# Tile 1 loaded two places earlier, and the opening of a macaron block in new instruction orders

## The chip, the cores and the metric

One core of one Trainium2 chip. The metric is the device time of one execution in microseconds (us), the median of several runs. The engines are TensorE (PE, with its weight loads as PEld), VectorE (DVE), ScalarE (ACT), GpSimd (POOL) and SyncE (SP), which only issues transfers here.

## The reference

`x` is 16 sequences of 256 tokens of 128 features, 4096 tokens in all. Three residual parts follow each other:

```python
x = x + 0.5 * ffn(layernorm(x))
x = x + attention(layernorm(x))      # layernorm again inside, with gamma and beta
x = x + 0.5 * ffn(layernorm(x))

def ffn(x):        # weights ternary (-1, 0, 1), one scale per output
    h = silu(x @ w1.T * s1) * (x @ w2.T * s2)      # 128 -> 512
    h = gelu(h @ h1.T * sh1)                       # 512 -> 512
    h = gelu(h @ h2.T * sh2)                       # 512 -> 512
    return h @ w3.T * s3                           # 512 -> 128

def attention(h):  # running sums along the sequence
    keys, values = h @ Wk.T + bk, h @ Wv.T + bv
    w = exp((keys @ Wka.T + bka) / sqrt(128)); w = w / cumsum(w)
    return cumsum(w * keys) * values
```

## The kernel before

The tokens are worked in 8 tiles of 512 (`TOK`). Each tile goes through the first ffn (steps T = 0 to 7), the attention, and the second ffn (T = 8 to 15), so there are 16 ffn tiles, worked by a software pipeline of 16 steps. All is held in SBUF. In step i TensorE works the second and third layers of tile i (`p2`, `p3`, 32 products of 128x128 by 512 columns each), the first layer of tile i+1 (`p1`, 16 products) and the last layer of tile i-1 (`p4`, 8 products). A hidden size of 512 is four chunks m = 0 to 3 of 128 rows; `p2.0` is output chunk 0.

Every activation is split into a high part, rounded to the matmul's format (`high`, ScalarE, `act_hi`), and the rest (`low`, VectorE, `act_lo`), and every product is made twice, once for each. Weights are used in a copy cast to that format (`hi`). As this is exact only for weights without low bits, the kernel *looks* at all weights (`bits:h1.0` is the look at quarter 0 of `h1`: a maximum on VectorE, L801, or a sum on ScalarE, L713, over the low 16-bit halves), collects the looks in a flag in three steps (`raise` on VectorE L811, `sum` on TensorE L556 and L564, `copy` to an integer on VectorE L816), and TensorE loads the flag (L655) and branches (L656) ahead of each of its parts "first", "second" and "rest".

The first layer of one chunk runs: `p1.m` on TensorE writes a gate and an up bank; `tanh.m` on ScalarE (L684) reads the gate; `gate.m` (L855) and `up.m` (L867) on VectorE make the product in `full1`; `high1.m` (ScalarE L689) and `low1.m` (VectorE L877; in the opening chunks 1 and 2 on GpSimd, L375) make its two parts. The layer norm of a tile is `stats` (L825), `aggr` (L832) and `veps` (L839, L840) on VectorE, a power on GpSimd (L362, L364), `z` on ScalarE (L726), four transposes `t` on TensorE (L462) and `t` on ScalarE and VectorE, which make `xn_hi` and `xn_lo`. Of gelu, `gelu2.m` (L701) reads the bank of `p2.m`. `dt` adds the result of `p4` to the residual in `xt_sb`. The fold (L625, L626) multiplies two attention weights together once.

Each engine executes its queue in order. The orders are written out by hand as strings: `START` (tile 0's norm, then its first layer), `SECOND_LAYER` (TensorE's products of `p2` of tile 0 one by one: `p2ahi.0` is input chunk a, high part, output chunk 0), `FIRST_STEP` (the rest of step 0), `ORDER` (three kinds of steps with attention and, as its fourth entry, one without, used in steps 1 and 14) and `LAST_STEP`. A tile is counted `AHEAD`: `stats`, `aggr`, `veps`, `zwait` and `z` belong to tile i+2, `t`, `p1`, `tanh`, `gate`, `up`, `high1` and `low1` to tile i+1. An order decides only when an instruction is issued; its semaphore waits stay as they are. So what stands behind a waiting instruction waits too.

In tile 0's second layer the banks are `gate_ps` and `up_ps`, so `p2ahi.0` waits for `gate.0`, `p2ahi.1` for `up.0`, `p2ahi.2` for `gate.1` and `p2ahi.3` for `up.1`; in tile 1's first layer `p1.2` waits for `gelu2.0` and `gelu2.1`, and `p1.3` for `gelu2.2` and `gelu2.3`, which read its banks.

Transfers of the opening are issued from SP and from ACT: on SP the first half of tile 0, `w1`, `h1.0`, `h1.2`, half of `h1.3`, tile 1 (`xload(1, 2, s_x1t)`), `h2`, `w3`; on ACT the other half of tile 0, `w2`, the vectors, `h1.1` and the other half of `h1.3`.

Of the kernel before, what the change touches and what calls it, by code (L numbers as in the profile page):

```python
# [10 lines left out]
ACT = mybir.ActivationFunctionType  # L11
# [22 lines left out]
        "t vec:s1 bits:h1.1 bits:h1.3 tanh.0 tanh.1 tanh.2 high1.0 tanh.3 high1.1 zwait z.0 z.1 high1.2 bits:h2.0 "  # L34
        "high1.3 1:t",
# [3 lines left out]
        "flag:copy1 bits:h1.0 t vec:scales bits:h1.2 stats flag:raise2 aggr gate.0 veps flag:copy2 up.0 gate.1 "  # L39
        "up.1 low1.0 gate.2 up.2 gate.3 up.3 bits:h2.1 low1.3 1:t",  # L40
# [8 lines left out]
)  # L49
FIRST_STEP = {  # L50
# [52 lines left out]
def macaron_block(nc, x, xt, w1t, w2t, h1t, h2t, w3t, wkt, wkat, wvt, wkn, vecs, out, seq):  # L103
# [895 lines left out]
```

## Time and profile before

| | us |
|---|---|
| time before, median of 3 runs (376.67 to 377.38) | 376.67 |
| the profiled execution | 376.7 |
| its span, first to last instruction | 374.9 |
| busy: TensorE, weight loads | 368.0, 291.9 |
| busy: VectorE, ScalarE, GpSimd | 321.9, 314.1, 52.6 |

The page gives the busy share of each engine and its slices. TensorE is busy in all but the first and the last slices; its granted clock is 0.998 of full speed as a mean. Matmuls are pipelined, so one lasts longer (0.39 us) than the step from one to the next. In a row of the timeline, the bracket behind an instruction tells how long its engine was idle before it and what ended that.

### The profile page before, as it was taken

What the parts mean: (1) busy time and instruction counts of PE and PEld (TensorE: products, weight loads), DVE (VectorE), ACT (ScalarE), POOL (GpSimd) and SP (SyncE); (2) the same over time, 40 slices, a digit from 0 to 9 for tenths busy, and PEclk for the clock granted to TensorE, in tenths of its full rate; (3) what the DMA queues carried; (4) which work ended last, traced back from release to release, by engine and by line L of the source; (5) the groups of instructions that cost most, each with busy time, mean ns of one, the idle gap of its engine ahead of it and who ended that gap; (6) DMA issues with size and microseconds to landing.
All of it is one profiled execution on the core that took longest, in us unless ns stands there. A gap on an engine that the chain in (4) does not pass through costs nothing.

```text
span 374.9 us, 5278 instructions
## 1 busy us (share of the span) xinstructions
PE 368.0 (98%) x1662; PEld 291.9 (78%) x1662; DVE 321.9 (86%) x713; ACT 314.1 (84%) x549; POOL 52.6 (14%) x67
## 2 busy tenths in 40 slices
PE   7999999999999999999999999999999999999996
PEld 2678888787787877778788787778877778788885
DVE  5898787999999799999988999989799999976733
ACT  4999699989977999798699979967998998686763
POOL 3531101202101202201021120102101210020000
PEclk9999999999999999999999999999999999999999
DMA  7760000000000000000000000000000000000001
GB/s 246 277 265 1 2 0 0 1 2 1 0 2 0 1 2 2 2 0 1 2 0 1 2 1 28 2 28 1 2 29 0 0 30 1 30 1 28 2 0 58
DMA packets 4494, 9.81 MB, mean 26 GB/s; under 512 B 625, under 2 KB 1905, under 8 KB 4209
## 3 DMA queue, kind: packets, MB, share of 16 engines
q1 hardware_dynamic: 3744, 8.65, 6.3%
q10 hardware_dynamic: 720, 0.80, 0.6%
q8 instruction: 15, 0.25, 0.2%
q14 instruction: 15, 0.11, 0.1%
HBM read 7.35 MB, written 2.10 MB: 25 GB/s over the span
## 4 chain that ended last, share of the span: by engine, by line
PE 95%; DMA 2%; DVE 1%; SPq 1%; issue 0%; ACT 0%; ACTq 0%
PE hid_ps L449 60%; PE gate_ps L449 8%; PE y_ps L449 7%; PE up_ps L449 7%; PE xt_ps L462 3%; DMA x_sb<-x 2%; PE y_ps L462 2%; PE xt_ps L632 2%; PE xt_ps L629 2%; PE xt_ps L635 2%; PE up_ps L507 1%; PE gate_ps L507 1%; DVE gate L855 0%; PE xt_ps L449 0%; DVE xt_sb L924 0%
## 5 line engine op out<-in xcount | busy, mean ns | idle before, releaser
L449 PE MATMUL hid_ps<-act_hi,hi_h 128*128 128x512 f32 x480 | 195.6, 408 | 0.0
L449 PE MATMUL hid_ps<-act_lo,hi_h 128*128 128x512 f32 x480 | 186.8, 389 | 0.0
L877 DVE TENSOR_TENSOR act_lo<-full,act_hi 128x512 fp32r<-128x512 f32 x185 | 122.2, 683 | 26.8 <-ACT act_hi L708 24.3
L701 ACT ACTIVATE full<-hid_ps,vec 128x512 f32<-128x512 f32 x123 | 84.4, 686 | 34.9 <-PE hid_ps L449 31.2
L449 PEld LDWEIGHTS hid_ps<-act_hi,hi_h 128*128 128x128 f32 x480 | 90.1, 188 | 22.4 <-issue 4.1
L449 PEld LDWEIGHTS hid_ps<-act_lo,hi_h 128*128 128x128 f32 x480 | 90.2, 188 | 22.1 <-issue 4.3
L708 ACT ACTIVATE act_hi<-full 128x512 fp32r<-128x512 f32 x127 | 78.5, 630 | 2.3
L362 POOL TENSOR_TENSOR rstd<-veps,half 128x4 f32<-128x4 f32 x24 | 35.2, 1467 | 272.5 <-DVE veps L840 272.5
L855 DVE SCALAR_TENSOR_TENSOR gate<-tanh,gate_ps 128x512 f32<-128x512 f32 x60 | 40.6, 679 | 9.2 <-ACT tanh L684 8.6
L684 ACT ACTIVATE tanh<-gate_ps,s_half 128x512 f32<-128x512 f32 x60 | 40.8, 686 | 8.2 <-PE gate_ps L449 8.2
L867 DVE SCALAR_TENSOR_TENSOR full<-up_ps,s_half,gate 128x512 f32<-128x512 f32 x60 | 44.2, 742 | 0.9
L689 ACT ACTIVATE act_hi<-full 128x512 fp32r<-128x512 f32 x60 | 37.3, 621 | 0.2
L940 DVE RECIPROCAL rcsum<-csum 128x256 f32<-128x256 f32 x16 | 27.9, 1743 | 0.0
L449 PE MATMUL gate_ps<-xn_hi,hi_w 128*128 128x512 f32 x59 | 24.7, 419 | 0.0
L726 ACT ACTIVATE z<-y_ps,nmr,rstd 128x128 f32<-128x128 f32 x64 | 24.0, 460 | 0.8 <-POOL nmr L364 0.8
L449 PE MATMUL y_ps<-act_hi,hi_w 128*128 128x512 f32 x60 | 24.2, 403 | 0.0
L449 PE MATMUL y_ps<-act_lo,hi_w 128*128 128x512 f32 x60 | 23.5, 392 | 0.0
L449 PE MATMUL gate_ps<-xn_lo,hi_w 128*128 128x512 f32 x59 | 23.0, 390 | 0.0
L449 PE MATMUL up_ps<-xn_lo,hi_w 128*128 128x512 f32 x59 | 23.0, 390 | 0.0
L449 PE MATMUL up_ps<-xn_hi,hi_w 128*128 128x512 f32 x59 | 23.0, 390 | 0.0
L825 DVE BATCH_NORM_STATS2 stats<-y_ps 128x6 f32<-128x128 f32 x64 | 14.2, 285 | 0.0
L462 PE MATMUL xt_ps<-ident,z 128*128 128x128 f32 x90 | 13.6, 273 | 0.0
(159 smaller groups left out, 397.8 us busy)
## 6 DMA issues: line engine op xcount, KB each, us to landing
xt_sb<-xt SPq DMA_DIRECT2D x1, 2048.0 KB, 10.9
out<-xt_sb SPq DMA_DIRECT2D x7, 256.0 KB, 2.0
x_sb<-x SPq DMA_DIRECT2D x1, 1536.0 KB, 6.6
raw_h<-h2t SPq DMA_DIRECT2D x4, 256.0 KB, 7.3
raw_h<-h1t SPq DMA_DIRECT2D x2, 256.0 KB, 5.9
raw_w<-w2t ACTq DMA_DIRECT2D x1, 256.0 KB, 4.0
raw_w<-w1t SPq DMA_DIRECT2D x1, 256.0 KB, 3.8
raw_h<-h1t ACTq DMA_DIRECT2D x1, 256.0 KB, 6.7
```

Source lines behind the costliest of these rows:

```text
L362: eng.tensor_tensor(rstd[:, :], veps[:, :], half[:, :], ALU.pow).then_inc(s_pow, 1)
L449: mm = eng.matmul(ps, w, a, start=(first and n == 0), stop=(last and n == len(seq_) - 1))
L462: mm = eng.transpose(dst[:, j * P:(j + 1) * P], src[:, j * P:(j + 1) * P], ident[:, :])
L684: eng.activation(tanh_b[m % 2][:, :], gate_home(T, m)[:, :], ACT.Tanh, scale=s1_half[:, m:m + 1]).then_inc(s_tanh, 1)
L689: eng.activation(act_hi[first_act(T)][:, m, :], full1[m % 2][:, :], ACT.Copy).then_inc(s_hi[1], 1)
L701: eng.activation(full23[m % 2][:, :], home23(n, T, m)[:, :], ACT.Gelu, scale=col("sh1" if n == 2 else "sh2", m)).then_inc(s_gelu[n], 1)
L708: eng.activation(act_hi[n][:, m, :], full23[m % 2][:, :], ACT.Copy).then_inc(s_hi[n], 1)
L726: zz = eng.activation(z[:, j * P:(j + 1) * P], norm_blk(kind, t, j), ACT.Identity, bias=nmr[:, j:j + 1], scale=rstd[:, j:j + 1])
L855: eng.scalar_tensor_tensor(gate_b[m % 2][:, :], tanh_b[m % 2][:, :], 1.0, gate_home(T, m)[:, :], ALU.add, ALU.mult).then_inc(s_gate, 1)
L867: eng.scalar_tensor_tensor(full1[m % 2][:, :], up_home(T, m)[:, :], s12_half[:, m:m + 1], gate_b[m % 2][:, :], ALU.mult, ALU.mult).then_in ...
L877: eng.tensor_tensor(act_lo[a][:, m, :], full[m % 2][:, :], act_hi[a][:, m, :].bitcast(F32), ALU.subtract).then_inc(s_lo[n], 1)
L940: eng.reciprocal(rcsum[:, b], csum[:, b]).then_inc(s_rc, 1)
```

## The change

Five things, all of them in the order of instructions; no operation is added or taken away.

1. SP issues the load of tile 1 behind `h1.0`, ahead of `h1.2` and half of `h1.3`.
2. `START`: VectorE looks at `h1.0` and makes the scales ahead of copy 1 and `t`; the statistics of tile 1 come ahead of the look at `h1.2`; `raise2` comes behind `gate.0`. ScalarE makes its scale ahead of `t` and looks at `h1.3` behind `tanh.0`, at `h2.0` behind `tanh.1` and at `h2.1` (which was VectorE's) ahead of `high1.3`; `z` is cut in two halves around `high1.1` and `tanh.3`.
3. `SECOND_LAYER`: the products of tile 0's second layer in another order; one of them (`p2clo.3`) moves behind the sum of flag 3.
4. `FIRST_STEP`: TensorE makes the fold behind `p1.3`; ScalarE's `tanh.2` and `tanh.3` come earlier; VectorE's `veps` comes ahead of `low2.0`.
5. `ORDER`, fourth entry (steps 1 and 14): `p4` behind `p2.3`; on ScalarE `t` ahead of `gelu2.0`; on VectorE `stats` first and `dt` late.

```diff
@@ -31,36 +31,36 @@
     ),
     "ACT": (
         "hi:w1 hi:w2 zwait z",
-        "t vec:s1 bits:h1.1 bits:h1.3 tanh.0 tanh.1 tanh.2 high1.0 tanh.3 high1.1 zwait z.0 z.1 high1.2 bits:h2.0 "
-        "high1.3 1:t",
+        "vec:s1 t bits:h1.1 tanh.0 bits:h1.3 tanh.1 bits:h2.0 tanh.2 high1.0 zwait z.0 high1.1 tanh.3 z.1 high1.2 "
+        "bits:h2.1 high1.3 1:t",
     ),
     "DVE": (
         "stats aggr veps bits:w1 bits:w2 norm",
-        "flag:copy1 bits:h1.0 t vec:scales bits:h1.2 stats flag:raise2 aggr gate.0 veps flag:copy2 up.0 gate.1 "
-        "up.1 low1.0 gate.2 up.2 gate.3 up.3 bits:h2.1 low1.3 1:t",
+        "bits:h1.0 vec:scales flag:copy1 t stats bits:h1.2 aggr gate.0 flag:raise2 veps up.0 flag:copy2 gate.1 "
+        "up.1 low1.0 gate.2 up.2 gate.3 up.3 low1.3 1:t",
     ),
 }
 
 
 SECOND_LAYER = (
-    "p2ahi.0 p2ahi.1 p2ahi.2 p2ahi.3 p2alo.1 p2alo.3 p2bhi.3 p2alo.0 p2alo.2 p2bhi.0 p2bhi.2 t p2blo.0 p2bhi.1 "
-    "p2blo.1 p2blo.3 p2chi.0 p2blo.2 p2clo.0 p2dhi.0 p2chi.1 p2chi.2 p2clo.1 p2dlo.0 p2chi.3 p2dhi.1 p2clo.3 "
-    "p2clo.2 p2dlo.1 flag:sum3 p1.0 p2dhi.2 p2dhi.3 p1.1 p2dlo.2 p2dlo.3"
+    "p2ahi.0 p2ahi.2 p2ahi.3 p2ahi.1 p2alo.2 p2alo.1 p2alo.0 p2alo.3 p2bhi.1 p2bhi.2 p2bhi.0 p2bhi.3 t p2blo.0 "
+    "p2blo.2 p2chi.0 p2chi.2 p2blo.1 p2chi.1 p2clo.0 p2clo.2 p2dhi.0 p2clo.1 p2dlo.0 p2blo.3 p2chi.3 p2dhi.1 "
+    "p2dlo.1 flag:sum3 p1.0 p2dhi.2 p1.1 p2clo.3 p2dlo.2 p2dhi.3 p2dlo.3"
 )
 FIRST_STEP = {
-    "PE": "p1.2 0:fold p1.3 p3.0 p3.1 p3.2 p3.3",
-    "ACT": "bits:w3 bits:h2.3 gelu2.0 high2.0 gelu2.1 tanh.0 high2.1 tanh.1 gelu2.2 gelu2.3 high2.2 high1.0 high2.3 tanh.2 "
-           "high1.1 gelu3.0 tanh.3 high3.0 high1.2 gelu3.1 high3.1 high1.3 gelu3.2 zwait z gelu3.3 high3.2 high3.3",
-    "DVE": "bits:h2.2 flag:raise3 stats aggr flag:copy3 low2.0 gate.0 low2.1 gate.1 up.0 up.1 "
-           "low2.2 low2.3 low1.0 gate.2 low1.1 up.2 gate.3 veps up.3 low3.0 low3.1 low1.2 low1.3 0:fold low3.2 "
-           "low3.3",
+    "PE": "p1.2 p1.3 0:fold p3.0 p3.1 p3.2 p3.3",
+    "ACT": "bits:w3 bits:h2.3 gelu2.0 high2.0 gelu2.1 tanh.0 high2.1 tanh.1 gelu2.2 gelu2.3 high2.2 tanh.2 high2.3 "
+           "tanh.3 high1.0 zwait high1.1 gelu3.0 high3.0 high1.2 gelu3.1 high3.1 high1.3 gelu3.2 z gelu3.3 high3.2 "
+           "high3.3",
+    "DVE": "bits:h2.2 flag:raise3 stats aggr flag:copy3 veps low2.0 gate.0 low2.1 gate.1 up.0 up.1 low2.2 low2.3 "
+           "gate.2 low1.0 low1.1 up.2 gate.3 up.3 low3.0 low1.2 low3.1 low1.3 0:fold low3.2 low3.3",
 }
 ORDER = {
     "PE": (
         "p2.0 a:u t p2.1 p2.2 p1.0 p1.1 p2.3 p1.2 a:t p4 p1.3 a:logits u p3.0 p3.1 a:keys p3.2 p3.3",
         "p2.0 t b:u p2.1 p2.2 p1.0 p1.1 a:values p2.3 b:t p4 p1.2 p1.3 u b:logits p3.0 p3.1 b:keys p3.2 p3.3",
         "p2.0 p2.1 t p2.2 p4 p1.0 p1.1 p2.3 b:values p1.2 p3.0 u p3.1 p1.3 p3.2 p3.3",
-        "p2.0 t p2.1 p2.2 p1.0 p1.1 p4 p2.3 p1.2 p1.3 p3.0 p3.1 p3.2 p3.3",
+        "p2.0 t p2.1 p2.2 p1.0 p1.1 p2.3 p4 p1.2 p1.3 p3.0 p3.1 p3.2 p3.3",
     ),
     "ACT": (
         "gelu2.0 high2.0 t gelu2.1 high2.1 gelu2.2 tanh.0 high2.2 tanh.1 a:zwait a:z tanh.2 gelu2.3 high1.0 "
@@ -71,8 +71,8 @@
         "gelu3.3 high3.3 zwait z",
         "gelu2.0 t gelu2.1 high2.0 high2.1 gelu2.2 high2.2 tanh.0 tanh.1 gelu2.3 high2.3 high1.0 tanh.2 gelu3.0 "
         "high3.0 high1.1 gelu3.1 tanh.3 high3.1 high1.2 gelu3.2 high3.2 high1.3 zwait z gelu3.3 high3.3",
-        "gelu2.0 t gelu2.1 high2.0 tanh.0 high2.1 tanh.1 gelu2.2 high2.2 gelu2.3 high1.0 high2.3 high1.1 tanh.2 "
-        "zwait tanh.3 gelu3.0 high3.0 gelu3.1 high1.2 high3.1 gelu3.2 high3.2 high1.3 z gelu3.3 high3.3",
+        "t gelu2.0 gelu2.1 high2.0 high2.1 gelu2.2 tanh.0 tanh.1 high2.2 gelu2.3 high1.0 high1.1 tanh.2 high2.3 "
+        "gelu3.0 tanh.3 high3.0 gelu3.1 zwait high3.1 high1.2 gelu3.2 high3.2 high1.3 z gelu3.3 high3.3",
     ),
     "DVE": (
         "a:stats low2.0 a:aggr t a:veps low2.1 gate.0 up.0 gate.1 up.1 low2.2 gate.2 low1.0 low2.3 dt up.2 low1.1 "
@@ -82,8 +82,8 @@
         "low1.3 b:recip.0 low3.2 b:recip.1 low3.3 b:weight",
         "t b:weight_keys low2.0 b:pool low2.1 dt gate.0 low2.2 up.0 gate.1 b:values low2.3 b:dt gate.2 up.1 stats "
         "low1.0 low3.0 aggr up.2 gate.3 veps low1.1 up.3 low1.2 low3.1 low1.3 low3.2 low3.3",
-        "t stats gate.0 low2.0 up.0 gate.1 up.1 aggr low2.1 veps dt low2.2 low2.3 low1.0 gate.2 gate.3 up.2 low1.1 "
-        "low3.0 up.3 low1.2 low3.1 low3.2 low1.3 low3.3",
+        "stats t aggr low2.0 low2.1 gate.0 up.0 gate.1 up.1 veps low1.0 low2.2 low1.1 low2.3 gate.2 up.2 gate.3 "
+        "low3.0 up.3 low1.2 low3.1 low1.3 dt low3.2 low3.3",
     ),
 }
 
@@ -322,9 +322,9 @@
             eng.dma_start(x_sb[:, 0:TOK // 2], x[:, 0:TOK // 2]).then_inc(s_x0, 16)
             eng.dma_start(raw["w1"][:, :], w1t).then_inc(s_w1, 16)
             eng.dma_start(part(raw, "h1", 0), h1t[:, 0:HID]).then_inc(s_h1[0], 16)
+            xload(1, 2, s_x1t)
             eng.dma_start(part(raw, "h1", 2), h1t[:, 2 * HID:3 * HID]).then_inc(s_h1[2], 16)
             eng.dma_start(h1_end(raw["h1"], 0), h1_end(h1t, 0)).then_inc(s_h1[3], 16)
-            xload(1, 2, s_x1t)
             for k in range(MC):
                 eng.dma_start(part(raw, "h2", k), h2t[:, k * HID:(k + 1) * HID]).then_inc(s_h2[k], 16)
             eng.dma_start(raw["w3"][:, :], w3t).then_inc(s_w3, 16)
```

## Rows read from the trace of the kernel before

**Rows 1.** Busy time by stretch: bounds, length, engines (instructions), clock, DMA share, GB/s.

```profile
13.66:26.52 12.86, 12.80 (x58) 9.80 (x59) 12.27 (x28) 12.43 (x26) 5.84 (x7) 1.00 0.83 309
26.52:360.00 333.48, 333.48 (x1499) 267.44 (x1498) 295.70 (x640) 287.55 (x499) 41.04 (x44) 1.00 0.02 6
```

**Rows 2.** Chain that ended last: start us, length us, what.

```profile
3.06 7.05 DMA x_sb<-x
...
26.68 9.08 PE hid_ps L449 x40
35.77 0.44 PE xt_ps L462 x4
```

**Rows 3.** Timeline of TensorE: start us, us, what [idle before <-releaser].

```profile
8.41 0.36 PE L478 MATMUL gate_ps<-xn_hi,hi_w 128*128 128x256 f32 x1 [0.56 <-ACT xn_hi L762]
...
9.20 0.28 PE L478 MATMUL gate_ps<-xn_lo,hi_w 128*128 128x256 f32 x1
...
11.13 0.19 PE L564 MATMUL y_ps<-ones,inexact 128*1 128x1 f32 x2 [0.59 <-DVE inexact L811]
11.25 0.50 PE L449 MATMUL hid_ps<-xn_hi,hi_w 128*128 128x512 f32 x1
...
13.66 0.47 PE L507 MATMUL gate_ps<-act_hi,hi_h 128*128 128x512 f32 x1 [0.22 <-ACT act_hi L689]
...
25.05 0.38 PE L625 MATMUL xt_ps<-wka,wk_rows 128*128 128x128 f32 x2
...
25.52 0.47 PE L449 MATMUL gate_ps<-xn_hi,hi_w 128*128 128x512 f32 x1
```

**Rows 4.** Timeline of VectorE, 7 to 12 us, same columns.

```profile
7.27 0.14 DVE L816 CAST flag_i<-hid_ps 1x1 int32<-1x1 f32 x1
7.34 0.66 DVE L801 TENSOR_REDUCE bits<-raw_h 128x1 f32<-128x512 uint16 x1
...
10.14 0.87 DVE L825 BATCH_NORM_STATS2 stats<-x_sb 128x6 f32<-128x128 f32 x4 [0.65 <-DMA x_sb<-x]
10.93 0.14 DVE L811 TENSOR_REDUCE inexact<-bits 128x1 f32<-128x6 f32 x1
...
11.35 0.65 DVE L855 SCALAR_TENSOR_TENSOR gate<-tanh,gate_ps 128x512 f32<-128x512 f32 x1
```

**Rows 5.** Timeline of SyncE, issue of the quarter h1.2.

```profile
2.12 0.43 SPq L325 DMA_DIRECT2D raw_h<-h1t  x1
```

**Rows 6.** DMA issues between 2.5 and 2.7 us: KB each, us to landing.

```profile
raw_h<-h1t SPq DMA_DIRECT2D x1, 256.0 KB, 6.6
...
raw_h<-h1t SPq DMA_DIRECT2D x1, 128.0 KB, 6.0
```

**Rows 7.** TensorE's load of flag 1, L655, 7 to 8 us.

```profile
L655 PEldq TENSOR_LOAD <-flag_i x1: 495/495/495, 7.4 to 7.4; - x1
```

**Rows 8.** Timeline of ScalarE, same columns as rows 3.

```profile
7.88 0.38 ACT L762 ACTIVATE xn_hi<-y_ps 128x256 fp32r<-128x256 f32 x1
...
9.67 0.64 ACT L713 ACTIVATE csum<-raw_h 128x512 f32<-128x512 uint16 x1
...
10.30 1.25 ACT L684 ACTIVATE tanh<-gate_ps,s_half 128x512 f32<-128x512 f32 x2
...
14.81 1.64 ACT L726 ACTIVATE z<-x_sb,nmr,rstd 128x128 f32<-128x128 f32 x4
...
24.70 0.68 ACT L701 ACTIVATE full<-up_ps,vec 128x512 f32<-128x512 f32 x1
```

**Rows 9.** Timeline of GpSimd, low1.2 of tile 0.

```profile
17.05 1.30 POOL L375 TENSOR_TENSOR act_lo<-full,act_hi 128x512 fp32r<-128x512 f32 x1 [0.78 <-ACT act_hi L689]
```

**Rows 10.** Warm-up: weight loads at first, then the last matmuls.

```profile
2.94 0.13 PEld L642 LDWEIGHTS y_ps<-ones 128*1 128x1 f32 x1 [0.30 <-issue]
3.36 0.13 PEld L642 LDWEIGHTS y_ps<-ones 128*1 128x1 f32 x1 [0.30 <-issue]
...
6.51 0.59 PE L642 MATMUL y_ps<-ones 128*1 128x256 f32 x2
```

## The prediction

> **What bounds the kernel now.** I read the stages first, then TensorE's own rows, then the engines that feed it. From 26.5 us to the last tile TensorE is never idle: 333.48 us busy out of 333.48, at a granted clock of 1.00 [rows 1]. A moved step there can gain only if it ends a wait that no row shows. The chain of waits says the same and gives the pace: 40 products of 512 columns in 9.08 us, 0.227 each [rows 2]. Time can come or go only in the opening. Between 13.66 us (first product of the second layer, `p2ahi.0`) and 26.52 (first of `p3.0`) stand 32 products of the second layer and 16 of tile 1's first layer, 48 x 0.227 = 10.90, with four transposes (0.44 [rows 2]), the flag sum (11.13 to 11.25, 0.12) and the fold (25.05, about 0.4 [rows 3]): 11.86. The stage takes 12.86 [rows 1], so about 1.0 us of it is waiting, in pieces of 0.1 to 0.2. Before it TensorE waits twice in the open: 0.56 us for `xn_hi` at 8.41, and 0.59 at 11.13 for `inexact`, which VectorE makes only after the statistics of tile 1 [rows 3]. Those waited for their data: 0.65 us idle until 10.14, when the transfer of 7.05 us from 3.06 landed [rows 2, 4]. That is the wait the change aims at.
>
> I follow the change until `p3.0` starts and add the difference to the median, 376.67 (the profiled execution took 376.7, with a span of 374.9, so the two are one).
>
> **The load.** Tile 1 is issued two places earlier, in the slot of 2.12 us, whose transfer landed after 6.6 us, at 8.7; the half quarter issued right behind it took 6.0, and landed at 8.6 [rows 5, 6]. I take 8.7 for tile 1. The three transfers together are the same bytes, so the last of them lands at 10.1 as the last does now. Bounds for tile 1: 8.6 to 10.1. The Trainium skill ("DMA: Bandwidth & Descriptors", "Queues, rings and completion order") says that completion is not FIFO per issuing engine; here the half quarter issued second did land first by 0.1, so the page and these rows agree, and by that rule alone the place in the queue would promise nothing (the second rival has its price).
>
> **Flag 1 comes later.** Copy 1 runs on VectorE at 7.27 and the look at h1.0 behind it (0.66) [rows 4]. Now the look and the two small scales come first. An instruction here starts 0.07 before the one in front of it ends (7.27+0.14 against 7.34). So: look 7.27, scales 7.86 and 7.93, copy 8.00 to 8.14 instead of 7.41. TensorE reads the flag with a load of 0.495 us that begins as the copy ends [rows 7], and then branches; today `p1.0` starts 8.41-7.41 = 1.00 after the copy's end. New: 9.14, that is +0.73. The profile names `xn_hi` as the releaser; its first half is read from 7.85 on and the second ends at 7.88+0.38 = 8.26 [rows 8]. If that end was the limit, `p1.0` needs of the flag no more than what remains when 8.26-7.41 is taken off, and could start as early as 8.14+0.44 = 8.6, +0.17. Bounds +0.17 to +0.73. I take +0.73, as the load fills the gap.
>
> **Looks and tanh.** ScalarE reaches `tanh.0` at 10.30 today because it first looks at h1.3 (9.67 to 10.30, 0.63) [rows 8]. The new order puts that look behind. The first gate tile is ready 9.20+0.28-8.41 = 1.07 after `p1.0` starts [rows 3], so `tanh.0` starts (0.04 behind TensorE's end) at 9.14+1.07+0.04 = 10.25: no change, since what the order gives the late flag takes. VectorE: `t` to 8.8, statistics 8.75 to 9.6, look at h1.2 (landed between 8.7 and 10.1) ends by 10.2 to 10.8, aggregates 0.33, done by 11.0 at the latest; `gate.0` needs `tanh.0` (10.25+0.67) and starts at 10.95, 0.4 earlier than 11.35. But `raise2` now stands behind `gate.0` and needs the look at h1.3, which ScalarE makes after `tanh.0`: 10.25+0.57+0.63+0.09 = 11.55 (0.57 and 0.68 are the step and the length of a tanh: two take 1.25 [rows 8]; 0.09 is the last step to VectorE). It ran at 10.93 [rows 4]. So the sum of flag 2 is at 11.13+0.64 = 11.77 and `p1.2` starts at 11.89 instead of 11.25 [rows 3]: **one wait is replaced by another**, for VectorE's `raise2` as before, which stands behind ScalarE's look instead of a transfer. `p1.2` and `p1.3`, eight products and a restart of 0.1, end at 13.84. (Copy 2 stands behind `veps` and `up.0`; a pass like `gate.0`'s, 0.66, from 11.84 puts it at 12.50 to 12.64, ahead of `p1.3` at 12.92.)
>
> **Start of the second layer.** ScalarE: `tanh.1` 11.45, look at h2.0 12.02, `tanh.2` when `p1.2`'s gate tile is ready (11.89+0.34+0.39+0.04 = 12.66), `high1.0` 0.57 later at 13.23, ended 13.86. `p2ahi.0` follows 0.14 later as it does today: 14.00 instead of 13.66, **+0.34**.
>
> **Through the second layer.** The new order takes four products of high chunk 0, then four of low chunk 0, and asks for later chunks about 0.5 us later than they come (high 1: 13.23+0.54, two blocks of `z` at 0.385, a pass of 0.63, so ready at 15.2; asked for at 15.9). 27 products, the transposes and 0.17 of restarts bring TensorE to the sum of flag 3 at 14.00+6.13+0.45+0.17 = 20.8. What feeds it: ScalarE is now full from `tanh.0` on, and `high1.2`, behind `tanh.3` (0.57) and the other half of `z` (0.77), starts at 16.43, against 16.35 today, at the end of `z` (14.81+1.64 [rows 8]); GpSimd's `low1.2`, which starts as that ends (17.05) and takes 1.30 [rows 9], moves by 0.08, with it VectorE's `low1.3`, `t`, the last look and `raise3`, and the sum stands at about 20.98. Today it is at 21.14 [rows 3] with one product more behind it (0.23): **+0.07**. So the 0.34 is absorbed by waits that were there. The looks at h2.0 and h2.1 on ScalarE cost 0.63 each and fill its pauses before `tanh.2` and `high1.3`; VectorE loses one look of 0.66 in a place where it waits for GpSimd, so nothing comes of it. Without that cover each would cost 0.6.
>
> **The end of the stage.** `p1.3` of tile 1 needs `gelu2.3`, 24.70+0.68 = 25.38 today [rows 8]; the fold (25.05) runs inside this wait and `p1.3` starts at 25.52 [rows 3]. Now the fold stands behind `p1.3`. By the steps above the last product of the second layer starts at 23.96, `gelu2.3` runs 24.53 to 25.21 behind `gelu2.2`, TensorE is ready for `p1.3` at 25.10 and gets it at 25.36. Its four products take 0.99 with the restart, the fold then 0.4 in the open: `p3.0` at 26.78 against 26.52, **+0.26**. An earlier `gelu2.3` can save at most the 0.26 of that wait; a later one costs one for one. `veps` of tile 2 (0.14) is far from anybody's need.
>
> **Steps 1 and 14.** `t` before `gelu2.0` on ScalarE delays the gelu by one copy (0.6); its bank is needed 8 x 0.227 = 1.8 us later. `p4` behind `p2.3` swaps two groups, both ready; `dt` late on VectorE has until the next step. I cost them at nothing, bounds -0.1 to +0.1 each: TensorE's busy row [rows 1] leaves no more to win.
>
> **Sum:** 376.67+0.26 = 376.93, say **376.9**. With the flag's lower bound (+0.17) about 0.2 less comes out of `p2ahi.0` and the rest, 376.7; with h1.2 and the small restarts each 0.1 late, 377.2.
>
> **Rivals.** (1) *The waits inside the second layer go.* The new order fits the chunks, `p1.0` comes at the lower bound, `tanh.0` at 9.7 and `raise2` as early as the look at h1.3 allows (landing 10.1, so 11.0). Then `p2ahi.0` is 0.2 early and up to the 1.0 of waiting falls away: 376.67-1.2 = 375.5. For it: that 1.0 is there. Against: ScalarE's row of work from `tanh.0` to `high1.2` has no pause left, and GpSimd's two slow chunks hang on it. Chance 0.11. (2) *The load does not come forward*, the slower side. The order has the statistics in front of `gate.0` whatever lands. They may begin at 10.95-0.33-0.60-0.79 = 9.23 and no later; if tile 1 lands at 10.1, `gate.0` is at 11.83, `raise2` 0.85 later than I have it, and the second layer with it, only some of it absorbed: 376.93+0.85 = 377.8. It decides from a landing of 9.2. For it: transfers issued together land together. Against: the slot landed at 8.7. Chance 0.11. (3) *The clock falls.* TensorE now rests about 1.3 us before `p1.0` (7.85 to 9.14) and 0.7 before the flag sum. The warm-up rows show the lower level: weight loads of its 256-column steps 0.43 apart, against 0.21 later [rows 10]. If 3 us of products ran at it, 1.5 would be lost: 378.4. Against: TensorE rests 0.56 and 0.59 today and the granted clock stays 1.00 [rows 1, 3], and the warm-up brings it up just before. Chance 0.05. The Trainium skill ("TensorE: Matmul & The Clock Gate", "Why this matters for your kernels") warns of pauses between bursts longer than these; by its rule the clock holds.
>
> **Chances.** Forecast 0.73, rivals as given. A change of 0.2% (0.75 us) is about what a measurement of this kernel can tell from none; the runs shown lie 0.7 apart. The forecast's own range 376.2 to 377.4 is within that but for its upper edge. Faster 0.12, same 0.71, slower 0.17. The range takes in rival 2 and reaches part of the way to rival 1: 375.9 to 377.8.
>
> **What would show it.** After: `stats` of tile 1 at 8.7 to 8.8 with no idle time before it; the flag load at 8.2 and `p1.0` at 9.1; `tanh.0` at 10.25; TensorE's wait for `inexact` about 0.6 again, `p1.2` at 11.9; `p2ahi.0` at 14.0; the flag sum 3 at 21.0; `p1.3` waiting for `gelu2.3`; `p3.0` at 26.8; afterwards the same 348 us. Wrong: `p1.0` at 8.6, `stats` at 10, a clock below 1.00 before 20 us, or idle time on TensorE in steps 1 or 14.

## The result, and the profile after

The changed kernel takes **377.67 us** in the median of 20 runs (377.20 to 378.76). The kernel before, timed in turn with it on the same chip, takes 376.71 (20 runs, 376.27 to 377.49). The medians are 0.96 apart. The ratio, over all runs, is 1.0023, 95% interval 1.0017 to 1.0029, and that is 0.87 us: slower, and by about the 0.2% that the prediction named as what can be told (the interval reaches to both sides of it). The forecast was +0.26.

The profiled execution took 377.27, with a span of 375.5 (before: 376.7 and 374.9). So the two traces are 0.57 apart, not 0.87, and this one is among the changed kernel's quicker executions (fifth of 20). I first read what the two traces show, and come back to the remainder behind the experiments.

TensorE of the changed kernel in the opening, from its timeline (start us, length us, what, idle time before it and what ended it), which answers to [rows 3]:

```profile
9.29 0.35 PE L478 MATMUL gate_ps<-xn_hi,hi_w 128*128 128x256 f32 x1 [1.51 <-ACT xn_hi L762]
...
12.01 0.19 PE L564 MATMUL y_ps<-ones,inexact 128*1 128x1 f32 x2 [0.59 <-DVE inexact L811]
12.13 0.50 PE L449 MATMUL hid_ps<-xn_hi,hi_w 128*128 128x512 f32 x1
...
14.25 0.70 PE L507 MATMUL gate_ps<-act_hi,hi_h 128*128 128x512 f32 x2
...
21.18 0.19 PE L564 MATMUL xt_ps<-ones,inexact 128*1 128x1 f32 x2
...
25.56 0.47 PE L449 MATMUL gate_ps<-xn_hi,hi_w 128*128 128x512 f32 x1
...
26.57 0.38 PE L625 MATMUL xt_ps<-wka,wk_rows 128*128 128x128 f32 x2
26.93 0.47 PE L449 MATMUL hid_ps<-act_hi,hi_h 128*128 128x512 f32 x1
27.24 0.39 PE L449 MATMUL hid_ps<-act_lo,hi_h 128*128 128x512 f32 x1
```

Read the starts from top to bottom: `p1.0` 9.29 (8.41 before), `p1.2` 12.13 (11.25), `p2ahi.0` 14.25 (13.66), flag sum 3 21.18 (21.14), `p1.3` 25.56 (25.52), `p3.0` 26.93 (26.52). The delay is +0.88, +0.88, +0.59, +0.04, +0.04, +0.41: the way through the second layer has become shorter than the delay it inherits (sum 3 also has one product of 0.23 fewer in front of it), and the fold behind `p1.3` makes a new delay. The wait for `inexact` is 0.59 again, as before: a wait replaced by another of the same length.

VectorE's timeline shows by what ([rows 4] before):

```profile
8.19 0.14 DVE L816 CAST flag_i<-hid_ps 1x1 int32<-1x1 f32 x1
...
9.05 0.86 DVE L825 BATCH_NORM_STATS2 stats<-x_sb 128x6 f32<-128x128 f32 x4
...
10.23 0.69 DVE L801 TENSOR_REDUCE bits<-raw_h 128x1 f32<-128x512 uint16 x1 [0.32 <-DMA raw_h<-h1t]
...
11.19 0.69 DVE L855 SCALAR_TENSOR_TENSOR gate<-tanh,gate_ps 128x512 f32<-128x512 f32 x1
11.80 0.16 DVE L811 TENSOR_REDUCE inexact<-bits 128x1 f32<-128x6 f32 x1
```

The statistics of tile 1 start at 9.05 without idle time, 1.09 ahead of the 10.14 of before: tile 1's transfer now landed at 8.83. That half of the change works. But `raise2` (L811) stands behind `gate.0` and runs at 11.80, where it ran at 10.93. The new idle time on this engine is 0.32 before the look at `h1.2`, which now lands behind tile 1, at 10.21 (8.69 before). That look and the two small steps behind it end at 11.22 and `tanh.0` at 11.16: two chains reach `gate.0` (11.19) together, one from the landing of `h1.2`, one from flag 1.

ScalarE's timeline ([rows 8] before):

```profile
7.87 0.20 ACT L738 ACTIVATE s_half<-vec 128x4 f32<-128x4 f32 x1 [0.67 <-DMA vec<-vecs]
...
10.47 0.69 ACT L684 ACTIVATE tanh<-gate_ps,s_half 128x512 f32<-128x512 f32 x1 [0.44 <-PE gate_ps L478]
11.05 0.62 ACT L713 ACTIVATE csum<-raw_h 128x512 f32<-128x512 uint16 x1
...
24.73 0.68 ACT L701 ACTIVATE full<-up_ps,vec 128x512 f32<-128x512 f32 x1
```

`tanh.0` waits for the gate tile (0.44), the look at `h1.3` (L713) comes behind it, and on its end hangs `raise2`. The first row is one I had not reckoned with: the scales of the layer stand first on ScalarE and wait 0.67 for `vec`, which in this execution landed 0.8 later than in the one before.

The busy time by stretch (bounds, length, then busy us and instructions of the five engines, granted clock, DMA share, GB/s) answers to [rows 1]:

```profile
14.25:26.93 12.68, 12.60 (x59) 9.68 (x59) 11.37 (x28) 12.20 (x27) 7.55 (x9) 1.00 0.83 314
26.93:360.00 333.07, 333.07 (x1498) 266.93 (x1497) 295.72 (x636) 286.44 (x498) 40.23 (x42) 1.00 0.02 6
```

The second stage is 12.68 long instead of 12.86. Behind 26.93 TensorE is busy all the time, as before, and what is left over, 375.5 - 26.93, is 348.6 against 348.4: steps 1 and 14 hold no new idle time. About half of those 0.2 is the restart behind the fold: the second product of `p3.0` follows the first by 0.31 (26.93 to 27.24), where it took 0.23 before.

### The profile page after: what moved, and what is told of

The parts are those of the page before. It is cut to its first block, busy times and chain, and to the rows that moved or that the text cites. A ratio compares the mean times of both kernels' runs of the same rounds, so it can differ in the third digit from the quotient of the medians.

```text
span 375.5 us, 5279 instructions
## 1 busy us (share of the span) xinstructions
PE 367.9 (98%) x1662; PEld 292.0 (78%) x1662; DVE 322.1 (86%) x712; ACT 313.6 (84%) x551; POOL 53.6 (14%) x67
## 4 chain that ended last, share of the span: by engine, by line
PE 96%; DMA 2%; ACT 1%; DVE 0%; issue 0%; ACTq 0%
PE hid_ps L449 61%; PE gate_ps L449 8%; PE y_ps L449 8%; PE up_ps L449 7%; PE xt_ps L462 3%; PE y_ps L462 2%; PE xt_ps L632 2%; PE xt_ps L629 2%; PE xt_ps L635 2%; DMA vec<-vecs 2%; PE gate_ps L507 1%; PE up_ps L507 1%; PE xt_ps L449 0%; DVE xt_sb L924 0%; PE gate_ps L478 0%
## 5 line engine op out<-in xcount | busy, mean ns | idle before, releaser
L449 PEld LDWEIGHTS gate_ps<-xn_hi,hi_w 128*128 128x128 f32 x59 | 11.1, 188 | 3.6 <-issue 1.0
```

Source lines behind the costliest of these rows:

```text
L449: mm = eng.matmul(ps, w, a, start=(first and n == 0), stop=(last and n == len(seq_) - 1))
```

## The experiments

**My theory**: the load works; the orders give it back, first by `raise2` behind `gate.0` and ScalarE's look, then by the fold in the open. **Rivals**: the late flag 1 is what costs; or the load itself does harm, by putting the last quarter of `h1` and what is queued behind it later. All ratios below are to the kernel before, timed on the same chip, with 95% intervals (the medians beside them are of other chips than those of the result, so the ratios are what to compare); "before" and "changed" name the kernel that the edit was made to.

### Flag 1 first again, twice

```diff
- ACT "vec:s1 t bits:h1.1 ...      + ACT "t vec:s1 bits:h1.1 ...
- DVE "bits:h1.0 vec:scales flag:copy1 t stats ...
+ DVE "flag:copy1 bits:h1.0 t vec:scales stats ...
```

> The changed kernel with copy 1 ahead of the look at h1.0 and of the scales again, on VectorE and ScalarE. Theory (the late flag 1 costs nothing by itself): p1.0 starts at 8.4 to 8.5 instead of 9.30, but the look at h1.2 still waits for its landing at 10.2, gate.0 stays at 11.1 to 11.2, raise2 at 11.7 to 11.8, p1.2 at 12.1, p3.0 at 26.9, and the time is that of the changed kernel, 1.002 of before. Rival (the late flag is the price): all of the opening moves forward by up to 0.8, p2ahi.0 to 13.5 and the time to that of before or below it, 1.000 or less.

1.0033 [1.0021, 1.0046], 377.92 in 5 runs. Its trace could not tell the theories apart, for a reason outside the edit: TensorE's granted clock stayed at its lower level (1.2 GHz) until 7.85 us after the start of the span. The warm-up's weight loads kept the spacing of the lower level, 0.43 [rows 10], up to then; two of them:

```profile
6.36 0.13 PEld L642 LDWEIGHTS y_ps<-ones 128*1 128x1 f32 x1 [0.30 <-issue]
6.79 0.13 PEld L642 LDWEIGHTS y_ps<-ones 128*1 128x1 f32 x1 [0.30 <-POOL rstd L362]
```

The sum of flag 1 came at 7.97 instead of 6.94, and `p1.0` at 9.36, where 8.4 to 8.5 was expected, although copy 1 stood first. So I ran the same kernel again.

> The changed kernel with copy 1 ahead of the look at h1.0 and of the scales again, once more, since in the first execution with a profile the clock rose only at 7.6 us and hid what the edit does. Theory (VectorE's look at h1.2 waits for its landing and gate.0 stands behind it): with the clock up at 5.1, p1.0 at 8.4 to 8.6, but gate.0 at 11.0 to 11.3, p1.2 at 11.9 to 12.2, p3.0 at 26.8 to 27.1, ratio 1.002. Rival (the late flag is the price): p2ahi.0 at 13.6 and ratio 1.000.

1.0035 [1.0022, 1.0048], 378.31 in 5 runs. Now the clock was up in time, and TensorE's and VectorE's timelines say what the edit does:

```profile
8.39 0.36 PE L478 MATMUL gate_ps<-xn_hi,hi_w 128*128 128x256 f32 x1 [0.56 <-ACT xn_hi L762]
...
12.09 0.19 PE L564 MATMUL y_ps<-ones,inexact 128*1 128x1 f32 x2 [1.57 <-DVE inexact L811]
```

```profile
9.33 0.87 DVE L825 BATCH_NORM_STATS2 stats<-x_sb 128x6 f32<-128x128 f32 x4 [0.45 <-DMA x_sb<-x]
10.41 0.69 DVE L801 TENSOR_REDUCE bits<-raw_h 128x1 f32<-128x512 uint16 x1 [0.20 <-DMA raw_h<-h1t]
...
11.31 0.66 DVE L855 SCALAR_TENSOR_TENSOR gate<-tanh,gate_ps 128x512 f32<-128x512 f32 x1
11.88 0.15 DVE L811 TENSOR_REDUCE inexact<-bits 128x1 f32<-128x6 f32 x1
```

`p1.0` starts 0.90 earlier than in the changed kernel, and the wait behind it is longer by about as much (1.57 for 0.59): the flag sum is at 12.09 against 12.01. What sets `gate.0` here is the look at `h1.2`, which waited for its landing at 10.38, and in front of it the statistics. So with these landings the late flag 1 costs nothing, and neither set of runs is quicker than the changed kernel: as the price of the whole change that rival falls. It isn't free whatever lands: in `a_stats_late`, whose opening is that of the changed kernel, tile 1 and `h1.2` landed at 8.34 and 9.33, and `gate.0` waited 0.54 for `tanh.0`, which hangs on flag 1:

```profile
11.32 0.69 DVE L855 SCALAR_TENSOR_TENSOR gate<-tanh,gate_ps 128x512 f32<-128x512 f32 x1 [0.54 <-ACT tanh L684]
11.93 0.16 DVE L811 TENSOR_REDUCE inexact<-bits 128x1 f32<-128x6 f32 x1
```

### The load back at its old place, and the load alone

```diff
  changed, SyncE: xload(1, 2, s_x1t) again behind h1_end(...)
  before,  SyncE: xload(1, 2, s_x1t) moved to before part(raw, "h1", 2), nothing else
```

> The changed kernel with tile 1 loaded behind h1.2 and half of h1.3, as before. Theory (the statistics stand ahead of gate.0 whatever lands): statistics at 10.1 instead of 9.05, gate.0 at 11.9 instead of 11.19, raise2 at 12.4 instead of 11.80, p2ahi.0 at 14.8 to 14.9 instead of 14.25, p3.0 0.3 to 0.6 later than 26.93, ratio 1.003 to 1.004. Rival (the later landing of h1, 10.2 and 10.6 instead of 8.7 and 9.6, is what costs): p2ahi.0 at 13.7 to 14.0 and a ratio of 1.000.

1.0026 [1.0015, 1.0037], 377.73 in 8 runs. VectorE's timeline:

```profile
10.12 0.87 DVE L825 BATCH_NORM_STATS2 stats<-x_sb 128x6 f32<-128x128 f32 x4 [1.22 <-DMA x_sb<-x]
...
11.80 0.65 DVE L855 SCALAR_TENSOR_TENSOR gate<-tanh,gate_ps 128x512 f32<-128x512 f32 x1
12.37 0.15 DVE L811 TENSOR_REDUCE inexact<-bits 128x1 f32<-128x6 f32 x1
```

This is rival 2 of the prediction, built: tile 1 lands at 10.10, `gate.0` starts at 11.80 (I had worked out 11.83), `raise2` at 12.37, 0.57 behind the changed kernel's 11.80, `p2ahi.0` at 14.81 against 14.25, `p3.0` at 27.49 against 26.93. In the trace the orders need the load. Over all runs the kernel is only 0.0003 from the changed one, well within the intervals, and not at the 1.003 to 1.004 expected. So the 0.56 of one trace is not seen in the ratios.

> The kernel before with nothing but the load of tile 1 moved forward. Theory (the flag needs all of h1, and the bytes in front of its last quarter are now more): the look at h1.2 waits on VectorE until 10.2 instead of starting at 8.81, statistics at 10.85, raise2 at 11.65 instead of 10.93, p1.2 at 11.95, p2ahi.0 at 14.3, ratio 1.001 to 1.002. Rival (an earlier tile 1 is a gain in itself): raise2 before 10.93, p2ahi.0 before 13.66, ratio 0.999 or less.

1.0013 [1.0004, 1.0022], 377.15 in 11 runs (376.13 to 377.63). Here trace and times part company. The profiled execution was the quickest of all, 376.13, and in it the transfers from `h1.0` on landed 0.2 to 0.8 sooner than in the trace of before, and tile 1 at 8.04; only the two put behind tile 1 landed later, `h1.2` at 9.07 (8.69 before) and half of `h1.3` at 9.41 (8.63):

```profile
9.10 0.69 DVE L801 TENSOR_REDUCE bits<-raw_h 128x1 f32<-128x512 uint16 x1
9.70 0.86 DVE L825 BATCH_NORM_STATS2 stats<-x_sb 128x6 f32<-128x128 f32 x4
10.48 0.14 DVE L811 TENSOR_REDUCE inexact<-bits 128x1 f32<-128x6 f32 x1
```

`raise2` at 10.48, `p2ahi.0` at 13.22, `p3.0` at 26.05. But the median of the runs is above that of before. So the ratio is as expected while the trace shows the rival's rows. The load alone gains nothing, and costs some 0.4 us; this one trace does not tell why (an estimate from all of them stands in the next part).

### The change in two halves

```diff
  b_start: before + the load + the new order of the opening (START)
  b_rest:  before + SECOND_LAYER, FIRST_STEP and ORDER
```

> The kernel before with two parts of the change alone: the load and the START orders. Theory (the loss is made in START, by raise2 behind gate.0 and behind ScalarE's look at h1.3): p1.0 at 9.2, raise2 at 11.8, p2ahi.0 at 14.2, p3.0 at 26.7 to 26.9, ratio 1.001 to 1.002. Rival (the loss is made by the fold and the orders of steps 0, 1 and 14): ratio 1.000.

1.0012 [1.0004, 1.0021], 377.26 in 11 runs. The profiled execution, 378.21, was the slowest of the 11: `h1.2` landed at 10.77, `raise2` came at 12.27 (11.8 expected) and `p3.0` at 27.77 (26.7 to 26.9 expected).

> The kernel before with the other three parts alone: SECOND_LAYER, FIRST_STEP and ORDER; load and START as before. Theory (only the fold in the open costs, 0.2 to 0.3, less what an earlier last product gives): p2ahi.0 at 13.7, flag sum 3 at 20.9, p3.0 at 26.6 to 26.8, ratio 1.000 to 1.0008. Rival (these orders carry the loss): p3.0 at 26.9 or later, ratio 1.0015 or more.

1.0011 [1.0003, 1.0020], 377.25 in 12 runs. The halves add up: 0.0012 + 0.0011 = 0.0023. And `b_start` is no slower than the load alone (1.0013). So the bill reads: the load 0.4 to 0.5 us, the new order of looks, flags and statistics on top of it about nothing, the second layer and step 0 about 0.4, the first and the last with an interval of 0.3 to either side, the middle one, a difference of two, with a wider one. The new order of the opening without the load and without the other parts was not run. TensorE's timeline of `b_rest`:

```profile
13.39 0.69 PE L507 MATMUL gate_ps<-act_hi,hi_h 128*128 128x512 f32 x2 [0.23 <-ACT act_hi L689]
...
26.00 0.38 PE L625 MATMUL xt_ps<-wka,wk_rows 128*128 128x128 f32 x2
26.36 0.47 PE L449 MATMUL hid_ps<-act_hi,hi_h 128*128 128x512 f32 x1
```

This execution began its second layer 0.27 ahead of that of before (13.39, 13.66) and `p3.0` 0.16 ahead (26.36, 26.52). By 105 us the lead is down to 0.02. So these orders lose about 0.25 in a trace, 0.11 of it up to `p3.0`.

### The fold between `p1.2` and `p1.3` again

```diff
- "PE": "p1.2 p1.3 0:fold p3.0 ...      + "PE": "p1.2 0:fold p1.3 p3.0 ...
```

> The changed kernel with TensorE's fold between p1.2 and p1.3 of tile 1 again. Theory (the fold ran inside the wait for gelu2.3 and now runs in the open): p1.3 stays at 25.5 to 25.6, p3.0 starts at 26.5 to 26.6 instead of 26.93, and 0.3 to 0.4 us come back, ratio 1.0012 to 1.0015. Rival (p1.3 is pushed back by the fold): p3.0 at 26.9 and the time of the changed kernel, 1.002.

1.0017 [1.0009, 1.0026], 377.28 in 12 runs (377.04 to 378.40): by the ratios 0.2 us below the changed kernel, by the medians 0.4. That is the right sense, but the intervals overlap. The profiled execution, 378.40, was the slowest of the 12, and VectorE's timeline shows something else:

```profile
21.08 0.17 DVE L811 TENSOR_REDUCE inexact<-bits 128x1 f32<-128x11 f32 x1
22.21 0.87 DVE L825 BATCH_NORM_STATS2 stats<-x_sb 128x6 f32<-128x128 f32 x4 [0.97 <-DMA x_sb<-x]
...
23.42 0.11 DVE L816 CAST flag_i<-xt_ps 1x1 int32<-1x1 f32 x1
```

`stats` of tile 2 stands between the raise of flag 3 and its copy, in the kernel before too. Here it waited 0.97 for its transfer, copy 3 behind it came at 23.42 (22.23 in the changed kernel), and TensorE waited 0.7 for the flag. `p3.0` was at 27.85, where 26.5 to 26.6 was expected. The transfer is that of tiles 2 to 7. Its row among the DMA issues (KB, us from issue to landing) in this kernel, issued at 14.07, and then in the changed one, issued at 13.91:

```profile
x_sb<-x SPq DMA_DIRECT2D x1, 1536.0 KB, 8.1
```

```profile
x_sb<-x SPq DMA_DIRECT2D x1, 1536.0 KB, 6.5
```

In eleven of the 14 traces it was issued between 12.67 and 13.91 and took 6.5 to 6.7; in three, issued at 14.07, 14.09 and 14.43, it took 8.1, 7.7 and 8.1 and landed near 22, when 21.2 would have been in time. All three are kernels with the load moved forward (three of nine; of the five traces without it none). The issue comes 0.08 behind the landing of `w3` in each trace, at 13.65 in the mean of the nine against 13.17 of the five.

### Statistics of tile 2 late, in both kernels, and with the fold

```diff
- DVE "bits:h2.2 flag:raise3 stats aggr flag:copy3 veps low2.0 ... low2.3 gate.2 ...
+ DVE "bits:h2.2 flag:raise3 flag:copy3 low2.0 ... low2.3 stats low1.0 aggr veps gate.2 ...
```

> The changed kernel with the statistics of tile 2 (stats, aggr, veps) taken from between raise3 and copy 3 and put behind low2.3 in step 0, where VectorE has room. Theory (in part of the executions tile 2 lands at 22 us instead of 20, copy 3 waits behind its statistics and p1.1 of tile 1 with it, 0.8 to 1.0 us): no such executions are left, the times above 377.9 go, median 376.9 to 377.2, ratio 1.0005 to 1.0013. Rival (the late landing is an accident of the traces and the loss is all in START): 377.5 to 377.8, ratio 1.002 as the changed kernel.

> The kernel before with the same edit. Theory (before has the same wait in fewer executions, its upper times near 377.1 to 377.5, and copy 3 comes 0.6 us earlier in all): median 376.2 to 376.6, ratio 0.9985 to 0.9995. Rival (before never meets that wait, and TensorE is not held by copy 3): ratio 1.000, or slower where tile 2's norm then comes late for z, TensorE's transposes at 35.8 moved back.

> The first of these with the fold between p1.2 and p1.3 again, as the earlier test of the fold was hidden by tile 2's late landing. Theory (the fold in the open costs what the wait for gelu2.3 gave): p3.0 starts 0.2 to 0.35 us earlier, counted from the flag sum 3, than without that (5.75 in the changed kernel), ratio 0.0005 to 0.0009 below the first. Rival: no difference.

1.0068 [1.0054, 1.0082]; 1.0035 [1.0023, 1.0047]; 1.0073 [1.0059, 1.0086]. All three slower than what they were made from, where the first two were expected to be quicker than that: copy 3 is indeed early (21.54), but the mean and variance of tile 2 now come late for its norm, and what is behind waits. The row of the waits of ScalarE in the first of them (total us, count, longest):

```profile
ACT act_hi_second L689 <- POOL nmr L364: 3.0, 1, 3.0
```

With it TensorE is idle for 1.5 us until 32.5. In the kernel before the same edit costs less (TensorE idle for 0.6 at 32.2): there `zwait` stands behind `gelu3.2`, not ahead of `high1.1` and `gelu3.0`, so the late norm holds up less of ScalarE's work. Up to `p3.0`, though, these two traces are the cleanest comparison of the fold's place. TensorE with the fold behind `p1.3`, then between:

```profile
21.32 0.19 PE L564 MATMUL xt_ps<-ones,inexact 128*1 128x1 f32 x2
...
25.68 0.47 PE L449 MATMUL gate_ps<-xn_hi,hi_w 128*128 128x512 f32 x1
...
27.05 0.47 PE L449 MATMUL hid_ps<-act_hi,hi_h 128*128 128x512 f32 x1
```

```profile
21.60 0.19 PE L564 MATMUL xt_ps<-ones,inexact 128*1 128x1 f32 x2
...
25.71 0.38 PE L625 MATMUL xt_ps<-wka,wk_rows 128*128 128x128 f32 x2
26.07 0.49 PE L449 MATMUL gate_ps<-xn_hi,hi_w 128*128 128x512 f32 x1
...
27.10 0.39 PE L449 MATMUL hid_ps<-act_hi,hi_h 128*128 128x512 f32 x1
```

From flag sum 3 to `p3.0` it is 5.73 and 5.50: the fold in the open costs **0.23** at that point, as it adds 0.34 between `p1.3` and `p3.0`, and had pushed `p1.3` back by 0.11 where it stood before. The full times of these two (379.53 and 379.75) do not show it: the wait at 32 us is longer in the second (1.9).

### Copy 3 alone ahead of the statistics

```diff
- DVE "... flag:raise3 stats aggr flag:copy3 veps low2.0 gate.0 ...
+ DVE "... flag:raise3 flag:copy3 low2.0 stats aggr veps gate.0 ...
```

> The changed kernel with copy 3 and low2.0 ahead of the statistics of tile 2, and nothing put off further than that: veps still comes ahead of gate.0, some 1.3 us later than in the changed kernel, long before z. Theory (in part of the executions of the changed kernel tile 2 lands at 22 instead of 20.4 and copy 3 waits behind its statistics): copy 3 at 21.5, p1.1 right behind p2dhi.2 whatever lands, p3.0 less flag sum 3 at 5.75 as in the trace of the changed kernel and not 6.4 to 6.55 as in the two traces with the late landing; times above 377.9 go, median 377.2 to 377.4, ratio 1.001 to 1.0018. Rival (START alone carries the loss and the late landing is rare): 377.5 to 377.8 and ratio 1.002 to 1.003.

1.0027 [1.0018, 1.0036], 377.93 in 12 runs: 377.73 to 378.21. The median is no better than the changed kernel's, and not the 377.2 to 377.4 expected, but the spread of its 12 runs is 0.5 where that of the changed kernel's 20 is 1.6. Nothing is above 378.21 (the changed kernel up to 378.76) and nothing below 377.73 (377.20). TensorE's and ScalarE's rows show what the lower end costs:

```profile
26.25 0.47 PE L449 MATMUL gate_ps<-xn_hi,hi_w 128*128 128x512 f32 x1 [0.57 <-ACT full L701]
```

```profile
25.41 0.69 ACT L701 ACTIVATE full<-up_ps,vec 128x512 f32<-128x512 f32 x1 [0.37 <-DVE act_lo L877]
```

With `stats` (0.86) ahead of `low2.1`, VectorE is late for ScalarE's `gelu2.3`, by which `p1.3` of tile 1 starts: 0.7 later than in the changed kernel. The slow end goes and the quick end goes with it.

### `gate.0` first, in the kernel before

```diff
- ACT "... bits:h1.1 bits:h1.3 tanh.0 tanh.1 ...
+ ACT "... bits:h1.1 tanh.0 bits:h1.3 tanh.1 ...
- DVE "... bits:h1.2 stats flag:raise2 aggr gate.0 veps flag:copy2 up.0 gate.1 ...
+ DVE "... bits:h1.2 gate.0 flag:raise2 up.0 flag:copy2 stats aggr gate.1 veps ...
```

> The kernel before with tanh.0 ahead of the look at h1.3 on ScalarE and, on VectorE, gate.0, raise2, up.0 and copy 2 ahead of the statistics of tile 1, so that VectorE works on tile 0 while it used to wait for tile 1. Theory (the wait for tile 1 is the price, and something else can stand in front of it): gate.0 at 10.3, p1.2 at 11.2, p2ahi.0 at 13.3, p3.0 at 26.2 to 26.6, ratio 0.999 to 1.000. Rival (VectorE is full from 10.1 on, so what is taken forward is given back at up.1): p2ahi.0 at 13.3 but waits behind it, p3.0 at 26.5 to 26.7, ratio 1.000.

1.0026 [1.0016, 1.0037], 377.71 in 8 runs, slower where 0.999 to 1.000 was expected. VectorE's timeline:

```profile
10.52 0.69 DVE L855 SCALAR_TENSOR_TENSOR gate<-tanh,gate_ps 128x512 f32<-128x512 f32 x1 [0.73 <-ACT tanh L684]
...
12.04 0.85 DVE L825 BATCH_NORM_STATS2 stats<-x_sb 128x6 f32<-128x128 f32 x4
...
13.22 0.66 DVE L855 SCALAR_TENSOR_TENSOR gate<-tanh,gate_ps 128x512 f32<-128x512 f32 x1
```

`gate.0` came 0.83 earlier than before and `p2ahi.0` 0.08 earlier (13.58), but the statistics, no longer in idle time, push `gate.1` to 13.22 (12.79 before) and everything of VectorE behind it: flag sum 3 at 21.79 (21.14), `p3.0` at 27.15. Between 10.2 and 20.7 us of the trace of before VectorE has one pause, 0.26 before 18.45; the place where statistics cost nothing is the gap of 0.65 before 10.14, and there the changed kernel does have them.

## Why the prediction was right, and where it was wrong

The places in the chain were right; the size at the end was too small by 0.6 us (0.87 for 0.26), of which the profiled execution shows 0.3 (0.57). 377.67 lies within the range 375.9 to 377.8, but outside the forecast's own 376.2 to 377.4. The range reached that far only because it took in the price of rival 2, which is not what happened in the trace of the changed kernel: that the range holds is in part luck.

- **The load.** Tile 1 landed at 8.83 (8.7 forecast), statistics at 9.05 without idle time (8.75). Right. Wrong is the sentence that the last of the three transfers lands at 10.1 "as the last does now", meant as a neutral term. Then nobody in the opening waited for `h1.2`; now the looks do. Over the traces the last transfer of this group lands at 10.36 in the mean with the load forward (nine, 9.41 to 11.15) and at 9.88 without it (five, 9.57 to 10.12). Here it was 10.62, and `h1.2`, for which 8.7 to 10.1 was allowed, came at 10.21. The Trainium skill ("DMA: Bandwidth & Descriptors", "Issuing engines are not separate DMA queues") says that transfers from all issuing engines run on the same 16 DMA engines and interleave; the traces agree: on ScalarE's queue nothing was moved, and yet in the two main traces its `h1.1` landed 0.42 later (9.28, 8.86 before) and its half of `h1.3` 0.50 earlier (9.14, 9.64). One pair could be scatter, but the means over the nine and the five move the same way: 9.16 against 8.62, and 9.19 against 9.40.
- **Flag 1.** Copy at 8.19 (8.00), `p1.0` at 9.29 (9.14); the 0.19 is `vec`, which landed at 7.85 and which I had not bounded. From the end of copy 1, 8.33, to `p1.0` it is 0.96, where I took 1.00. The upper bound was the right one: the flag's load sets it and not `xn_hi`, which the row names and which had ended at 8.62. The lower bound was worked out wrongly: it adds 0.44 to the copy's end, where its own numbers leave 8.41 - 8.26 = 0.15. It said that an earlier `p1.0` would give 0.2 of `p2ahi.0`; in `a_flag1_again`, with `p1.0` at 8.39, it gave nothing.
- **Looks and tanh.** `tanh.0` 10.47 (10.25), `gate.0` 11.19 (10.95), `raise2` 11.80 (11.55), `p1.2` 12.13 (11.89): all 0.15 to 0.25 late: 0.15 from `vec`, and 0.07 as `tanh.0` followed `p1.0` by 1.18 and not 1.11. The landing of `h1.2` would have held `gate.0` as long by itself. "One wait is replaced by another" holds: 0.59 and 0.59.
- **Start of the second layer.** 14.25 (14.00); +0.59 for +0.34, the same inherited 0.25.
- **Through it.** Sum 3 at 21.18 (20.98), with `raise3` bound by GpSimd's slow chunk as forecast. It starts at 17.33 (17.05 before), and takes 1.30. +0.59 became +0.04, or +0.27 when the product that now stands behind the sum is counted in front of it as before (+0.07 forecast). The prediction put this down to waits that absorb the delay. The traces show a shorter way and no cushion: see the table below.
- **End of the stage.** `gelu2.3` 24.73 (24.53), `p1.3` 25.56 (25.36), `p3.0` 26.93 (26.78). The fold takes 0.37 in the open (0.4). The forecast set 0.16 against it, as `gelu2.3` was to come earlier than the 24.70 of before, and got +0.26; `gelu2.3` came no earlier, and it is +0.41. The step left out the restart behind the fold: 0.31 instead of 0.23 for the next product, 0.08 more.
- **Steps 1 and 14.** No idle time in the trace, as forecast. From `p3.0` to the end of TensorE's last product it is 345.32 (345.14 before); 0.08 of the 0.18 is the restart, and the other 0.1 is within the bounds given.
- **Rivals.** Rival 2 did not come in the trace of the changed kernel. It was to decide from a landing of tile 1 at 9.2, and in three of the other eight traces with the load forward tile 1 landed at 9.31 to 9.72. Built on purpose (`a_load_back`) it had the forecast time of `gate.0`, and in the ratio no price beyond the changed kernel's. Rival 3 (the clock falls) did not come in this kernel either. Rival 1 was the quick side; no trace showed it.

**The step that failed** is the first one of the sum, that the profiled execution and the median are one. For the total that is so (376.7 and 376.67); for a landing it is not. The forecast took the landings of one execution as the kernel's. They scatter, tile 1 by 0.55 in the five traces without the load forward and by 1.7 in the nine with it, and the opening passes that on. The distance from `raise2` to `p3.0` doesn't depend on the landings. The first three traces have the second layer of before, the last three that of the changed kernel (a landing is the transfer's issue with its time to landing added):

| trace | tile 1 landed | `h1.2` landed | `raise2` | `p3.0` | distance |
|---|---|---|---|---|---|
| `before` | 10.12 | 8.69 | 10.93 | 26.52 | 15.59 |
| `b_stats_late` | 9.57 | 8.01 | 10.38 | 25.96 | 15.58 |
| `b_load_only` | 8.04 | 9.07 | 10.48 | 26.05 | 15.57 |
| `after` | 8.83 | 10.21 | 11.80 | 26.93 | 15.13 |
| `a_stats_late` | 8.34 | 9.33 | 11.93 | 27.05 | 15.12 |
| `a_load_back` | 10.10 | 8.71 | 12.37 | 27.49 | 15.12 |

So everything hangs on `raise2`, and the two openings differ in how it takes the landings. In that of before it follows tile 1 by 0.81 (10.93, 10.38, and 10.65 in `b_rest`); the row is that of `b_stats_late`:

```profile
10.38 0.14 DVE L811 TENSOR_REDUCE inexact<-bits 128x1 f32<-128x6 f32 x1
```

In the changed kernel it stands at the end of flag 1, first layer, `tanh.0`, look and `gate.0`, which add up to 11.55 with every landing in time; the earliest landings of an unaltered new opening (`a_stats_late`) gave 11.93. An early landing gives it nothing, and a late one still costs.

The pair of main traces shows this too small: that of before has the latest landing of tile 1 of its five, that of the changed kernel the earliest `raise2` of all with the new opening. An estimate with means instead: the five landings at 9.88, with 0.81 and 15.58 behind, put `p3.0` of before at 26.27. In the six traces with the load and the new opening as built `raise2` comes at 12.02 in the mean, which with 15.12 gives 27.14. That is 0.87 later, and with the 0.18 behind `p3.0` 1.0 to 1.1 for the change, against 0.87 and 0.96 measured. The traces are of kernels that differ further on, so this supports the reading and doesn't prove it. The forecast had 0.62 at `raise2`, 0.36 of it given back by the shorter way; the runs show 1.3 (10.69 and 12.02), 0.46 given back.

**What stays open.** First, what of the 0.4 of the load alone belongs to which landing. In its trace `raise2` came 1.41 behind the landing of `h1.2` (look, statistics, raise). With the 9.98 at which `h1.2` lands in the mean of the nine traces that gives 11.39, 0.7 later than the 10.69 above: an estimate, inside the measured interval of 0.15 to 0.83. The later issue of tiles 2 to 7 adds to it in some runs. In three of nine traces it took a landing past 21.2 and cost 0.5 to 1.1 up to `p3.0`; two of these were the slowest run of their kernel, the third the middle one of five, and moving copy 3 off this wait cut the upper end. How often it occurs in the changed kernel was not measured, and it can't be the reason that the quickest runs are slower too (377.20 against 376.27). Second, why the whole queue runs 0.5 later and scatters more when the same bytes are only in another order. Third, the last transfer of the output, issued behind TensorE's end, took 2.3 us in both main traces and 2.4 to 2.8 in eight others; this is in the time of every run, and why it varies is not known.

## What to carry to other kernels

A collective condition, such as a flag raised when all quarters have been looked at, needs the last of its inputs: pulling one transfer forward on a queue pushes the others back, so ask first who waits for those, and for what is queued behind them. When steps are reordered, ask not only where the wait is in this trace, but what the new chain is worth when its inputs come early: an order that puts three engines in series ahead of a flag, as here, takes away the quick runs. And keep a step that waits for a transfer out from between the raise and the copy of a flag, unless that pushes work off a full engine, as it did here.

## What the runs showed of the hardware

- **One trace of the first 10 us is one sample.** With the same warm-up the granted clock rose to full speed between 4.91 and 8.04 us after the start of the span in 14 traces (12 of them by 6.3). TensorE works on the warm-up from 2.13 on in each. In the two late ones (7.85 and 8.04) the sum of flag 1 came at 7.97 and 8.24, in the others at 6.51 to 7.36. A pause of 1.57 us behind the rise (`a_flag1_again`) did not bring it down: the granted clock of that trace is 1.00.
- **A transfer of 1536 KB takes 6.5 to 6.7 us when issued up to 13.91, and 7.7 to 8.1 when issued from 14.07 on.** A step of 1.1 to 1.6 us for 0.2 in the issue; what else is moving then was not separated.
- **The landings scatter more than the kernel.** The last of the three transfers in question landed between 9.57 and 10.12 in five traces, and between 9.41 and 11.15 in the nine with tile 1 two places earlier. The last output transfer of 128 KB took 2.3 to 2.8 us. Between the two, from `p3.0` to the end of TensorE's last product, the eleven traces without late statistics of tile 2 are 345.0 to 345.3 long.
- **The register load of a flag** takes the same time in each trace: that of flag 1 0.492 to 0.498 us in all 14, those of flags 2 and 3 0.31. From the end of copy 1 to the first product behind the branch it is 0.96 to 1.00.

```profile
L655 PEldq TENSOR_LOAD <-flag_i x1: 493/493/493, 8.4 to 8.4; - x1
```
